# Row loads tied to single scatter passes, and four smaller moves, in a two-layer kernel with routed experts

## What is computed

```python
xn = _layernorm(x, axis=-1)
x = x + _L0_attn_ref(xn, ...) + _L0_ffn_ref(xn, ...)   # linear attention; 32 experts, 8 per token, and a shared one
xn = _layernorm(x, axis=-1)
x = x + _L1_attn_ref(xn, ...) + _L1_ffn_ref(xn, ...)   # gated recurrence; 8 experts, 2 per token, and a shared one
# an expert:  combine[:, e] * ((silu(x @ wg.T) * (x @ wu.T)) @ wd.T), inner width 176
```

## Time and profile before

| | |
|---|---|
| median of three runs | 1035.14 us (1029.52 to 1038.2) |
| the profiled execution: its own time | 1039.11 us |
| the profiled execution: span from first to last instruction | 1037.3 us |
| busy: PE / PEld / DVE / ACT / POOL | 82% / 58% / 34% / 30% / 48% of the span |
| mean granted TensorE clock | 0.914 of full |
| chain that ended last, by engine | PE 39%, POOL 27%, issue 16%, DMA 10%, DVE 3%, ACT 2% |

### The profile page before, as it was taken

One profiled execution on the slowest core, in us unless ns is written; L12 is line 12 of the kernel. 1 busy time (PEld: TensorE's weight loads), 2 busy tenths in 40 slices (PEclk: granted clock), 3 DMA queues, 4 the chain that ended last, 5 costly groups with the idle time before them and its releaser, 6 DMA issues.

```text
span 1037.3 us, 15472 instructions
## 1 busy us (share of the span) xinstructions
PE 847.6 (82%) x3786; PEld 598.0 (58%) x3786; DVE 357.8 (34%) x1043; ACT 315.4 (30%) x847; POOL 500.2 (48%) x387
## 2 busy tenths in 40 slices
PE   2889988820588899999999999971598999999970
PEld 2647745610355566666666666640576567777760
DVE  3552256710122232232332323331543163344343
ACT  4322221100232233333333333320521223344440
POOL 4014677777354465566666666534306505333231
PEclk9989998975699899999999999995578999999995
DMA  9996332442698799998899999897802225333627
GB/s 355 419 413 229 108 109 102 146 150 108 217 240 247 170 185 237 215 185 184 188 184 183 189 183 185 186 247 136 219 0 98 97 59 92 65 62 64 113 31 172
DMA packets 108242, 175.71 MB, mean 169 GB/s; under 512 B 13344, under 2 KB 82592, under 8 KB 105160
## 3 DMA queue, kind: packets, MB, share of 16 engines
q1 hardware_dynamic: 71392, 120.35, 37.4%
q0 software_dynamic: 36768, 54.39, 28.4%
HBM read 94.50 MB, written 80.19 MB: 168 GB/s over the span
## 4 chain that ended last, share of the span: by engine, by line
PE 39%; POOL 27%; issue 16%; DMA 10%; DVE 3%; ACT 2%; SPq 1%; POOLq 0%; ACTq 0%; DVEq 0%
POOL accs L556 14%; POOL xg L547 12%; PE banks L850 11%; PE banks L876 8%; DMA accs<-yb,xb 7%; PE banks L835 2%; PE banks L693 2%; PE banks L861 2%; DMA xg<-blank_rows,blank_idx 2%; PE banks L675 2%; PE banks L717 2%; PE banks L666 1%; PE banks L618 1%; PE banks L923 1%; PE banks L627 1%
## 5 line engine op out<-in xcount | busy, mean ns | idle before, releaser
L556 POOL DMA_INDIRECT accs<-yb,xb x198 | 307.7, 1554 | 326.2 <-ACT yb L1132 229.9
L850 PE MATMUL banks<-wgu,xt 128*128 x636 | 235.4, 466 | 0.3 <-ACT xt L1120 0.3
L547 POOL DMA_INDIRECT xg<-tok,slot_int x160 | 159.6, 997 | 113.4 <-issue 60.7
L1517 DVE SCALAR_TENSOR_TENSOR hid<-sg,xb,banks 128x176 f32<-128x176 f32 x198 | 78.6, 397 | 386.4 <-ACT sg L1126 384.2
L876 PE MATMUL banks<-wd,ht 88*128 88x256 f32 x636 | 187.4, 389 | 23.0 <-issue 15.4
L1120 ACT COPY xt<-banks 128x256 f32<-128x256 f32 x198 | 73.7, 372 | 285.5 <-PE banks L835 285.5
L835 PE MATMUL banks<-cst,xb 128*128 128x128 f32 x396 | 108.2, 275 | 55.6 <-DMA xb<-xg 54.5
L876 PEld LDWEIGHTS banks<-wd,ht 88*128 88x128 f32 x636 | 98.6, 195 | 66.5 <-issue 42.3
L850 PEld LDWEIGHTS banks<-wgu,xt 128*128 128x128 f32 x636 | 97.9, 193 | 41.8 <-issue 27.2
L835 PEld LDWEIGHTS banks<-cst,xb 128*128 128x128 f32 x396 | 56.1, 143 | 98.3 <-DMA xb<-xg 55.8
L861 PE MATMUL banks<-cst,hid 128*88 128x128 f32 x396 | 108.8, 276 | 0.0
(11 more groups left out here) (208 smaller groups left out, 878.9 us busy)
## 6 DMA issues: line engine op xcount, KB each, us to landing
xb<-xg SPq DMA_DIRECT2D x198, 144.5 KB, 3.4
wd<-in_wdn SPq DMA_DIRECT2D x159, 176.0 KB
accs<-zeros SPq DMA_DIRECT2D x20, 544.0 KB, 16.1
wgu<-in_wgu SPq DMA_DIRECT2D x6, 1408.0 KB, 9.3
xg<-blank_rows SPq DMA_DIRECT2D x7, 1156.0 KB, 17.6
accs<-yb,xb POOLq DMA_INDIRECT x198, 5.1
wgu<-in_wgu SPq DMA_DIRECT2D x1, 2816.0 KB, 26.2
gu<-in_wgu SPq DMA_DIRECT2D x1, 2816.0 KB
```

Of the source, the lines that this page charges most:

```text
L547: pool.indirect_dma_start(xg[n], bass.IndirectOffsetOnAxis(ap=(slot_int1 if n else slot_int)[:, t, k:k + 1], axis=0), tokw[:, t, :], None)\
L556: pool.indirect_dma_start(accs[a], bass.IndirectOffsetOnAxis(ap=xb[:, g % RING, ROW_ID:ROW].bitcast(U32), axis=0), yb[:, g % YB_RING, :], ...
L850: mm = pe.matmul(bank[2 + g % 2][:, 0:2 * F0], xt[:, g % 2, k, :], w[:, bass.ds(expert[g], 1), k, :].rearrange("p a n -> p (a n)"), start= ...
L1517: v.scalar_tensor_tensor(out=hb_[:, g % 2, :], in0=sg[:, g % 2, :], scalar=weight, in1=bank[2 + g % 2][:, F0:2 * F0], op0=ALU.mult, op1=AL ...
```

## The change

- The scatter passes run from a token's lowest slot to its highest, and each of two semaphores counts every second pass. A token's n-th lowest slot belongs to an expert of number n or higher, so the rows of expert e are complete after the passes 0 to e. DVE works out from the table of experts how many passes each of the first 32 blocks needs (`block_needs`), and `block_rows` of these blocks reads two such numbers into registers and waits for them. The wait for all passes goes.
- SP asks for the rows of 4 blocks ahead of the loop (before: 12) and, in iteration g, for those of block g + 4 (before: g + 9). The ring keeps its 12 slots.
- The last scatter pass has the adds of the first five blocks between its DMAs; the ring of results `yb` has 8 slots instead of 4.
- The gate and up weights from the thirteenth expert on come one expert at a time, one in each iteration; before, four at a time.
- ACT norms all four chunks ahead of the first sigmoid; DVE places ahead of piece 5 of `route0`; SP begins the fills when the indirect stores that blank each expert's last chunk have landed.
- Between the layers ACT's queue loads accumulator 3 and SP's loads accumulator 2, and DVE adds both. At the end ACT's queue has half of the loads and stores. The second layer's first 34 blocks alternate between the two accumulators, the last five go to the second.

The diff, without declarations, the tiles' addresses and what only renames:

```diff
-RING, LAG = 12, 3
+RING, AHEAD = 12, 4
-WD_RING, YB_RING = 3, 4
+WD_RING, YB_RING = 3, 8
-ACCS1, BOTH1, LAST1 = 2, 12, 10
+ACCS1, LAST1 = 2, 5
-ACC_OF += [ACCS0 + (b % ACCS1 if b < BOTH1 else int(b >= NB1 - LAST1)) for b in range(NB1)]
+ACC_OF += [ACCS0 + (b % ACCS1 if b < NB1 - LAST1 else 1) for b in range(NB1)]
+PASS = 16 * NT
+CAREFUL = 32
+EARLY_ADDS, ADD_EVERY = 5, 3
...
             def block_rows(g):
                 n, b = layer(g)
+                if g < CAREFUL:
+                    counts = [sp.value_load(need[0:1, n_, g:g + 1], min_val=PASS, max_val=PASS * TOPK0 // 2)
+                              for n_ in range(2)]
+                    for n_ in range(2):
+                        sp.wait_ge(passes[n_], counts[n_])
+                elif g == CAREFUL:
+                    for n_ in range(2):
+                        sp.wait_ge(passes[n_], PASS * TOPK0 // 2)
                 if g >= RING:
                     sp.wait_ge(added_to[ACC_OF[g - RING]], 16 * (adds_before(g - RING) + 1))
                 sp.dma_start(rows_of(g), xg[n][b * P:(b + 1) * P, :]).then_inc(xb_in[g % RING], 16)
...
             experts_in(0)
+            sp.wait_ge(ends_blank, 16 * ENDS)
...
-            sp.wait_ge(scattered[0], 16 * SCATTERED[0])
-            for g in range(RING):
+            sp.wait_ge(needs_known, 1)
+            for g in range(AHEAD):
                 block_rows(g)
             experts_in(1)
             for g in range(NB0):
                 if g + WD_RING < NB0:
                     down_weights(g + WD_RING)
-                if g >= LAG and g - LAG + RING < NB0:
-                    block_rows(g - LAG + RING)
-                if g % 4 == 0 and 2 + g // 4 < len(W_CHUNKS):
-                    experts_in(2 + g // 4)
+                if g + AHEAD < NB0:
+                    block_rows(g + AHEAD)
+                if 2 + g // 4 < len(W_CHUNKS):
+                    expert_in(2 + g // 4, g % 4)
...
-            for k in range(TOPK0):
+            for n in range(TOPK0):
+                if n >= 2:
+                    pool.wait_ge(passes[n % 2], PASS * (n // 2))
+                if n == TOPK0 - 1:
+                    pool.wait_ge(filled, 16 * FILLED)
+                    pool.wait_ge(acc_st, 16 * BATCH)
                 for t in range(NT):
-                    scatter_rows(0, t, k)
-            pool.wait_ge(scattered[0], 16 * SCATTERED[0])
+                    scatter_rows(0, t, TOPK0 - 1 - n, passes[n % 2])
+                    if n == TOPK0 - 1 and t % ADD_EVERY == ADD_EVERY - 1 and t // ADD_EVERY < EARLY_ADDS:
+                        add_rows(t // ADD_EVERY)
...
-            for q in range(NBLK):
-                pool.wait_ge(sums_late[q], 16 * 2 * BATCH)
-                tiles = slice(4 * q, 4 * q + 4)
-                v.tensor_tensor(sum_a[:, tiles], sum_a[:, tiles], sum_b[:, tiles], ALU.add).then_inc(late_added, 1)
...
-            norm_std(0)
-            norm_apply(0)
-            for c in range(1, NBLK):
+            for c in range(NBLK):
                 norm_std(c)
                 norm_apply(c)
-                width_out(c - 1)
-                if c == 2:
-                    scores(0)
-            width_out(NBLK - 1)
+                if c == 1 or c == 2:
+                    width_out(c - 1)
+            scores(0)
+            width_out(2)
+            width_out(3)
...
+            act.wait_ge(added_to[3], 16 * adds_to(3))
+            for q in range(NBLK):
+                rows_by_chunk(sum_b, accs[3], slice(4 * q, 4 * q + 4), sums_late[q])
...
+            act.wait_ge(added_to[ACCS0 + 1], 16 * adds_to(ACCS0 + 1))
+            for q in range(1, NBLK, 2):
+                rows_by_chunk(fin_b, accs[ACCS0 + 1], slice(4 * q, 4 * q + 4), fin_in[q])
...
+            place(0)
             route0(0, 5)
             route0(1, 5)
-            place(0)
...
                 link(v.tensor_tensor(acc[:, tiles], acc[:, tiles], sum_a[:, tiles], ALU.add))
+                link(v.tensor_tensor(acc[:, tiles], acc[:, tiles], sum_b[:, tiles], ALU.add))
```

More of the change, by code:

```diff
@@ L146, in build @@
         BESIDE_AT = BUF_AT + 6144
[L147 removed]
+        SMALL_AT = BESIDE_AT + 15104
         main = region(ACC_AT, RING_AT)
@@ L220, in build @@
         over = early("over", [P, E0, NT])
+        passes_ = early("passes_", [1, 2, CAREFUL])
         a_nat = early("a_nat", [P, 4, D])
@@ L289, in build @@
         ends_blank = sem("ends_blank")
-        scattered = [sem(f"scattered{n}") for n in range(2)]
+        passes = [sem(f"passes{n}") for n in range(2)]
+        scattered = sem("scattered")
+        needs_known = sem("needs_known")
         acc_st = sem("acc_st")
@@ L429, in block_rows, with rows_by_chunk @@
                 sp.dma_start(rows_of(g), xg[n][b * P:(b + 1) * P, :]).then_inc(xb_in[g % RING], 16)
+            def rows_by_chunk(dst, src, tiles, done):
+                for b in range(BATCH):
+                    sp.dma_start(dst[b * CH:(b + 1) * CH, tiles, :], by_chunk(src, b)[:, tiles, :]).then_inc(done, 16)
             def blank_blocks(n, low, high):
@@ L435, in blank_blocks @@
                         .then_inc(xg_blank[n], 16)
-            def by_chunk(a, b):
-                return a[b * SEQ:(b + 1) * SEQ, :].rearrange("(i s) w -> s i w", s=CH)
-            def rows_by_chunk(dst, src, tiles, done):
-                for b in range(BATCH):
-                    sp.dma_start(dst[b * CH:(b + 1) * CH, tiles, :], by_chunk(src, b)[:, tiles, :]).then_inc(done, 16)
             tokens_in(0)
@@ L1162, in beside_tile1, with rows_by_chunk @@
                     v.activation(std[:, 0, :], rec_k[:], ACT.Sigmoid, scale=-1.0).then_inc(kq_act, 1)
+            def rows_by_chunk(dst, src, tiles, done):
+                for b in range(BATCH):
+                    act.dma_start(dst[b * CH:(b + 1) * CH, tiles, :], by_chunk(src, b)[:, tiles, :]).then_inc(done, 16)
+            act.wait_ge(added_to[3], 16 * adds_to(3))
+            for q in range(NBLK):
+                rows_by_chunk(sum_b, accs[3], slice(4 * q, 4 * q + 4), sums_late[q])
             norm_std(NBLK)
@@ L1228, in _ @@
                 block_back(NB0 + n, NB0, ALL_BLOCKS)
+            act.wait_ge(added_to[ACCS0 + 1], 16 * adds_to(ACCS0 + 1))
+            for q in range(1, NBLK, 2):
+                rows_by_chunk(fin_b, accs[ACCS0 + 1], slice(4 * q, 4 * q + 4), fin_in[q])
+            for q in range(1, NBLK, 2):
+                act.wait_ge(fin_added, q + 1)
+                for b in range(BATCH):
+                    act.dma_start(by_chunk(out, b)[:, 4 * q:4 * q + 4, :],
+                                  acc[b * CH:(b + 1) * CH, 4 * q:4 * q + 4, :]).then_inc(stored, 16)
         @block.vector
@@ L1362, in expert_table, with block_needs @@
                 v.tensor_copy((table1 if n else table)[0:1, 0:cols], bank[6][0:1, D:D + cols]).then_inc(table_done, 1)
+            def block_needs():
+                dve.wait_ge(table_done, 1)
+                e = table[0:1, 0:CAREFUL]
+                for low in (2, 4, 6):
+                    for n in range(2):
+                        at = passes_[:, n]
+                        if low == 2:
+                            last = v.tensor_scalar(at, e, float(low + n), None, ALU.is_ge)
+                        else:
+                            last = v.scalar_tensor_tensor(out=at, in0=e, scalar=float(low + n), in1=at,
+                                                          op0=ALU.is_ge, op1=ALU.add)
+                    link(last)
+                v.tensor_scalar(need[:], passes_[:], float(PASS), float(PASS), ALU.mult, ALU.add).then_inc(needs_known, 1)
             def shared_hidden(t):
@@ L1539, in _ @@
                 block_back(g, 0, NB0)
[L1540 to L1544 removed]
+            for q in range(NBLK):
+                dve.wait_ge(sums_early[q], 16 * 2 * BATCH)
+                tiles = slice(4 * q, 4 * q + 4)
+                last = v.tensor_tensor(acc[:, tiles], acc[:, tiles], tok[:, tiles], ALU.add)
+            link(last)
             def sum_up(c):
                 tiles = slice(4 * c, 4 * c + 4)
[L1549 removed]
+                dve.wait_ge(sums_late[c], 16 * 2 * BATCH)
                 link(v.tensor_tensor(acc[:, tiles], acc[:, tiles], sum_a[:, tiles], ALU.add))
+                link(v.tensor_tensor(acc[:, tiles], acc[:, tiles], sum_b[:, tiles], ALU.add))
                 norm_stats(NBLK + c)
```

44 lines of the change are left out of this document (21 added, 23 removed).

## The result

The changed kernel takes 1689.02 us, the median of four runs (1684.66 to 1692.29). The kernel before, run beside it, takes 1032.33 us (four runs, 1027.17 to 1038.2). The ratio is 1.636, with a 95% interval of 1.625 to 1.646. The profiled execution has a time of its own of 1687.89 us, a span of 1686.0 us and a mean granted clock of 0.741 (before: 1037.3 us and 0.914). The forecast was 1710.

The account below looks back on a forecast made before the run. PE set the pace at 2.50 us per block; late row requests would make it wait every block. Start 229, 158 periods 1106, register loads 42, last row loads 16 and rest 317 sum to 1710 us, range 1480 to 1850.

Parts of the forecast that it names:

- first down product ends: First layer's start: with SP waiting only for the needed passes, the first down product ends at 229.2, 50 us won.
- landing to turn: First layer's block loop: one weight load and a wake-up of PE, estimated at 0.34 us, about 0.5 at the low clock.
- turn to the end of the next down product: First layer's block loop: PE's work after the rows land, 1.95 us at full clock, 3.93 at the low level.
- period, without register loads: First layer, per block: 7.0 us, a third of blocks at 5.57 (full clock), two thirds at 7.71 (low clock).
- register loads, in all: Blocks 4 to 31: two register loads between down weights and rows add 28 * 1.5 = 42 us.
- the last three periods: End of the first layer: part of the 158 periods of 7.0 us that the sum counted.
- last seven row loads: End of the first layer: row loads beside loads of closed accumulators land in 5.0 instead of 2.7 us, 16 us in all.
- rest behind the first layer's last down product: Everything after the first layer's block loop: 335.4 us less 8 between the layers and 10 at the end, 317.
- The deciding step: First layer's loop: SP's load for block g + 4 is issued 0.04 us after PE needs it, in every iteration.
- the second rival: First layer's loop: low clock in all blocks, 158 * 7.71 = 1218 us, 1822 us in total; chance 0.17.
- The first rival: First layer's loop: same loop with the clock kept, 158 * 5.57 = 880 us, 1484 us in total; chance 0.15.
- The rival "faster": First layer: rows come in time after all and the early start pays, 974 us in total; chance 0.05.

## Why the prediction was right, step by step

| step | forecast | measured |
|---|---|---|
| first down product ends | 229.2 | 227.78 + 0.60 = 228.4 |
| down product's end to issue of the rows | 0.58 | 0.57 |
| issue to landing | 2.7 (2.1 to 3.5) | 2.7 median in the dense part |
| landing to turn | 0.34 to 0.5 | under 0.1 |
| turn to the end of the next down product | 1.95 or 3.93, on average 3.27 | 2.04 to 3.78, on average 3.54 in the dense part |
| period, without register loads | 7.0 | 6.82 |
| register loads, in all | 42 | 39, and 17 more for slower landings and bursts beside them |
| the last three periods | 21 | 6.6 |
| last seven row loads | 16 | about 4 (1297.9 to 1342.4, six periods of 7.42) |
| rest behind the first layer's last down product | 317 | 329.8 of the span, 331.7 of the own time |

**The deciding step held.** The reading of the earlier trace rows together, that a load for block g + 4 is issued when PE wants block g + 4, is what the trace shows in every period, and the distance put alone into the kernel before reproduces it. Landing time, taken between the earlier trace rows, was right: 2.7.

**Two terms of the period were off and cancelled.** Between landing and turn I allowed 0.34 us and more, an estimate with no row behind it. The turn at 903.82 is 2.73 behind the issue, and a landing takes 2.7: nothing measurable is left. On the other side the burst is slower than my mean, 3.54 instead of 3.27. That 6.82 lies so near to 7.0 is in part luck.

**The clock was mixed in a different way than I had it.** I took a third of the blocks at full clock and two thirds at the low one. By the trace, 75 of the 155 bursts behind a wait for rows stay at 0.50 to their end and take 3.78 us or near it; 66 rise in their last part, as the one shown, and take 3.4 to 3.75; 9 run at 1.00 throughout and take 2.04; 5 lie between. A burst of the first kind and one of the third:

```profile
243.02:246.80 3.78, 3.78 (x10) 2.53 (x11) 0.40 (x1) 0.59 (x2) 0.76 (x1) 0.50 0.33 122
536.68:538.72 2.04, 2.03 (x11) 1.53 (x12) 0.20 (x1) 0.59 (x2) 0.00 (x0) 1.00 0.35 45
```

So the low clock had the larger share, as forecast (of the four waits of the earlier trace rows the last, 2.71, also left the clock at 1.00, from 426.50 to 430.00, which I had not read), but much of it within bursts, and far fewer than a third of the blocks were at full clock. The Trainium skill, page TensorE: Matmul & The Clock Gate, section "HAM oscillation — how this bites in real kernels", has each burst behind a DMA wait begin cold, that is at the low clock; the trace agrees for most: 140 of the 155 begin below 1.00, 134 of them at 0.50, and 15 begin at 1.00. Where I let that rule make the whole of every block slow (the second rival, 1822), the trace agrees for the 75 only. The first rival, the clock kept, gave 1484, and the version with the three added products shows what that case is: 1473.

**Register loads.** Two of them take 230.35 - 228.56 - 0.40 = 1.39 us, 1.5 forecast. But the 29 periods that mostly carry them are 8.81 long, 1.99 more than the dense 6.82. The other 0.6 is mostly the landing, on average 3.14 instead of 2.66, and for the rest the burst, which stays at the low clock in 23 of the 29 and takes 3.74 on average instead of 3.54. 29 * 0.6 = 17 us were not in the sum. The pieces of the expert weights, issued behind the first 20 of these loads, don't lengthen the landing: with a piece behind them the rows land in 2.5/3.3/3.6 (230.4 to 399.7, 20 loads), without one in 2.5/3.3/3.5 (408.8 to 471.1, 8 loads). In this part POOL issues an add some 1.2 us ahead of the rows (407.65 and 408.75, 415.75 and 417.03) instead of 0.1 behind them (901.20 and 901.09); whether that is the cause was not tried.

**The end terms failed.** From 335.4 I took off 18, 8 between the layers and 10 at the end. Measured by the span, 1686.0 - 1356.17 = 329.8 against 1037.3 - 703.7 = 333.6: 4 us won. The timeline between the layers and the chain at the end, with the load that falls on it:

```profile
1345.81 0.48 PE L856 MATMUL banks<-cst,xb 128*128 128x128 f32 x1 [2.58 <-DMA xb<-xg]
...
1348.53 1.06 PE L897 MATMUL banks<-wd,ht 88*128 88x256 f32 x2
...
1355.04 1.13 PE L897 MATMUL banks<-wd,ht 88*128 88x256 f32 x4 [0.51 <-DVE ht L1561]
...
1363.13 7.97 ACTq L1186 DMA_DIRECT2D sum_b<-accs  x16
1364.79 7.82 SPq L456 DMA_DIRECT2D sum_a<-accs  x16
1372.78 1.23 DVE L1601 TENSOR_TENSOR acc<-acc,sum_a 128x1024 f32<-128x1024 f32 x1 [13.26 <-DMA sum_a<-accs]
```

```profile
1632.50 1.91 SPq L456 DMA_DIRECT2D fin_a<-accs  x4
...
1667.14 3.62 SPq L456 DMA_DIRECT2D fin_b<-accs  x8
...
1674.51 2.36 DVE L1779 TENSOR_TENSOR acc<-acc,fin_b 128x1024 f32<-128x1024 f32 x2 [11.02 <-DMA fin_b<-accs]
```

```profile
1632.80 11.80 DMA accs<-yb,xb
...
1663.21 3.91 DMA accs<-yb,xb
1670.33 8.72 DMA fin_b<-accs
```

- Between the layers I named the wrong accumulator: the last block adds to accumulator 2, so 3 closes first, and its load by ACT at 1363.13 gains little. The first sum comes 1372.78 - 1356.17 = 16.6 us behind the last down product, before 721.27 - 703.73 = 17.5. Beside ACT's load the first quarter of SP's, asked for from 1364.79 on, is there 8.0 us later, and POOL's issue was held until DVE's sums were done. 0.9 us won instead of 8.
- From the first of these sums to the landing of the last add it takes 1667.12 - 1372.78 = 294.3 us, before 1019.88 - 721.27 = 298.6: 4.3 us for the two links that I priced at 8.6. The 2 MB load of the accumulator that closes later now falls on the last adds, one of which takes 11.80 instead of 3.6 to 3.9. In the kernel before that load fell on an add further from the end (issued at 974.10, landed after 9.70).
- Loading on two queues issues the last pieces in 3.74 us instead of 7.42, but both queues' pieces land together: from the last add's landing to the first of DVE's last sums it takes 1674.51 - 1667.12 = 7.4 us, before 1024.36 - 1019.88 = 4.5, and to the end of the span 18.9 against 17.4. Faster issue was counted as if it were faster landing.

**Three periods too many, and luck in the sum.** The last row load is that of block 158, asked for behind the down product of block 154. Its turn, at 1345.81, is PE's last wait for rows in this layer. So there are 155 periods of the loop and not 158: behind the end of block 155's down product, 1348.53 + 1.06 = 1349.59, the last three take 1356.17 - 1349.59 = 6.6 us, where the sum has 3 * 7.0 = 21. The 155 periods, with the 42 and the 16, were to take 1143 us and took 1349.6 - 228.4 = 1121. These 22 and 14 us too many, against 15 too few at the ends, make up the 22 between 1710 and the 1687.9 of the profiled execution. The sum is nearer than its terms.

**The rival "faster".** It was worked out as 974, and the version with nine ahead is that case: 992.58. The start was priced rightly: its first down product ends at 229.76 + 0.59 = 230.3 instead of 279.2, and the last at 658.05 + 2.04 = 660.1 instead of 703.7, so 49 us won at the start and 5 given back by the end of the layer, where I had 50 and 15. What was missing are the 12 for the pieces and the 18 for the ends: the pieces come to nothing that can be measured, and behind the last down product 993.6 - 660.1 = 333.5 us follow, as before.

## What to carry to other kernels

How far ahead a queue asks for data is read from where its issue stands against the use: count the instructions of the waiting and the waited-for kind up to one moment of the trace, and compare that lead with the longest landing time there, less what the queue's own iteration takes more than the consumer's. A lead that falls below zero closes a loop whose period is the sum of issue, landing and use, and it costs the landing in every iteration; one block of lead was worth 611 of 657 us here. A clock that falls in each of these waits can then cost a third of the loss, and a few matmuls that nobody needs, put where PE waits, buy that part back until the wait itself is gone.

## What the runs showed of the hardware that I had not expected

- **A POOL-issued indirect DMA stands still beside DVE's additions of two large tiles.** The issue of an add, 1.55 us alone, took 4.88, 2.18 and 1.69 and ended 1.41 to 1.43 us behind the end of the additions of 128x1024 in float32 in three kernels. An issue that was under way when an addition began was in some cases not held: in the kernel before one at 695.70 took 1.55 beside an addition that began at 696.19. With six ahead one was: issued at 664.39, 0.21 us ahead of four additions back to back (664.60, 4.62 us), it took 6.25 and ended 1.42 behind them. What decides between the two was not found. The Trainium skill, page SBUF — State Buffer, section "Who interferes with whom", has a VectorE instruction with two inputs in SBUF lock a port against a GpSimd instruction that reads SBUF, and infers that the making of DMA descriptors is spared by such additions. The first half fits; for these indirect DMAs, which take their row numbers from SBUF, the second does not.
- **A 2 MB load lengthens a small accumulating add beside it threefold**, from 3.6 to 3.9 us to 11.80 and 11.72, in the two kernels where it fell on the last adds, and to 9.70 in the kernel before. Of the first two, 0.66 us is the issue, which took 2.21 instead of 1.55 and began beside an operation of DVE on two 128x1024 tiles (1632.40, 1.20 us).
- **More work made the kernel faster.** Three products per block that nobody reads took 216 us off 1689, by keeping the clock at 0.99 where it was 0.63 (500 to 800 us).
